# Attention's convolution as products of fp32r high and low parts, in a fused MoE, attention, MoE kernel

## The chip, the cores and the metric

The kernel runs on one NeuronCore of a Trainium2 chip. The metric is device time in microseconds (us) of one execution, lower is better. The engines are TensorE (PE in the profile, its weight loads PEld), VectorE (DVE), ScalarE (ACT), GpSimd (POOL) and SyncE (SP); each works through its own instructions in program order and waits on semaphores for the others.

## The reference

Input x has 2 x 2048 tokens of 256 floats. Three layers follow each other, each on a layer norm of x and each added to x:

```python
x = x + 0.5 * _L0_ffn_ref(_layernorm(x), gate_up_proj, down_proj, router_w)
x = x + _L0_attn_ref(_layernorm(x), conv_w, conv_b, wq, bq, wk, bk, wv, bv, wo, bo, proj_w, proj_b)
x = x + 0.5 * _L0_ffn_ref(_layernorm(x), gate_up_proj, down_proj, router_w)
```

The feed-forward layer is a mixture of 8 experts, two for each token. The attention layer starts with the part that is changed here, a causal convolution over three tokens from 256 channels to 3 x 64 (q, k, v):

```python
xp = jnp.pad(x, ((0, 0), (2, 0), (0, 0)))
qkv = lax.conv_general_dilated(xp, conv_w, window_strides=(1,), padding='VALID',
                               dimension_numbers=('NWC', 'WIO', 'NWC')) + conv_b
q, k, v = jnp.split(qkv, 3, axis=-1)
```

Then come 8 heads of 64 over blocks of 128 tokens with a causal mask, a softmax, an output product and a projection back to 256. All is float32.

## The kernel before

The tokens are 32 tiles of 128, and x stays in SBUF in `x_sb` throughout.

**Expert stages.** Tokens are routed to 71 slots of 128 rows. For each slot a row tile comes in by DMA, PE turns it, ACT copies the turned tile to `rowsT_hi` in the float format fp32r, DVE subtracts that from the exact value into `rowsT_lo`, and PE makes three products: high x high, high x low, low x high. The down product is made in the same way.

**Attention.** `turns(turn)` runs a software pipeline of turns i = -8 to 36, written out by hand for each engine, and every engine goes through its part of turn i in the order of the code. In turn i tile i gets its scores and exponentials, tile i-1 its turned probabilities and context product, tile i-2 its projection, tile i+3 is turned for the convolution, tile i+5 gets the last layer's expert sums (`add_experts`), and tiles from i-5 on are routed for the next expert stage. The convolution works on pairs of tiles. In an odd turn PE makes the q and k channels of the next pair (`qk_pair`, 6 products of 128 x 128 weights with 256 columns, the two channel halves times three taps), and in an even turn the v channels (`v_pair`, 64 weight columns each, the two halves side by side in the array). The moving operand is `xT`, a view into `tile_oh`: 256 columns and 2 further ones ahead of them, the halo, which DVE copies from the pair before. The weights are `conv_sb`, exact float32.

Names that the steps use, in the order in which they come in one turn:

- PE: conv (L1529 q and k, L1538 v), mask and scores into `SS` (L1546, L1551), `prT` = the probabilities turned (L1557), which waits for POOL's `norm`, tile i+3 turned into `A` (L1565), projection `G` (L1594), context `F` (L1605), q and k heads (L1615), v products (L1625), ranks (L1637).
- DVE: `qk` or `vst_lo` (L1236, L1240), four small steps of the rstd, `nmax` (L1259), the routing of `PICKS` turns, residual `x_sb` (L1268), `mhaT` (L1281), halo (L1287), `add_experts` (L934), `qkh` (L1295), `rec` (L1300), statistics (L1309, L1312), `compare` (L1172 to L1178).
- ACT: the rstd seed (L746), `vo`, `hT_sb`, `vst_hi` (L762), `prT` copies (L768), `xT` copy (L777), 8 exponentials (L783).
- POOL: `norm` (L658), which waits for `rec`; gathers of expert results (L666); sends of routed rows (L675).

`PICKS` = {9, 13, 17, 21, 25, ...} are the turns in which four tiles at once get their experts picked on DVE; `compare` comes at the end of the turn before. Ahead of the first turn PE runs `keep_clock(F, 44)`, 44 products that serve nothing but activity. `wprep` counts prepared weights, `first["tokens"]` says that the token table of the first expert stage is done.

## Time and profile before

| | |
|---|---|
| time, median of 3 runs | 769.83 us (769.14 to 770.52) |
| the profiled execution's own time | 768.44 us |
| its span, first to last instruction | 766.7 us |
| mean granted clock of TensorE | 0.959 of full speed |
| PE busy | 684.0 us (89%) |
| DVE busy | 519.3 us (68%) |
| ACT busy | 488.2 us (64%) |
| POOL busy | 336.3 us (44%) |

Starts are in us from the first instruction. The first layer's routing ends at about 80 us, its experts at 230, attention runs from 230 to about 550, then come the last routing and experts. A row of the timeline merges neighbouring instructions of one line ("x12"), and its length is then from the first start to the last end. Matmuls overlap in the pipeline, so a single one's length is longer than the step from one start to the next.

### The profile page before, as it was taken

How to read it: one execution, taken by the hardware profiler on the slowest of the kernel's cores; microseconds unless marked ns; L12 is line 12 of the kernel's file. 1: busy time of each engine (PE TensorE's matmuls, PEld its weight loads, DVE VectorE, ACT ScalarE, POOL GpSimd, SP SyncE). 2: the span in 40 equal slices, each digit the busy share in tenths (PEclk: the TensorE clock that was granted, in tenths of full speed). 3: DMA queues.
4: the chain of work that ended last, by engine and by line, in shares of the span. 5: the costliest groups of instructions: out<-in, count | busy, mean ns of one | idle time of the engine just before them, and what ended most of it. 6: DMA issues, size and time to landing. Idle time of an engine off the chain costs nothing.

```text
span 766.7 us, 19140 instructions
## 1 busy us (share of the span) xinstructions
PE 684.0 (89%) x5321; PEld 587.7 (77%) x5354; DVE 519.3 (68%) x1747; ACT 488.2 (64%) x1735; POOL 336.3 (44%) x361
## 2 busy tenths in 40 slices
PE   4999899999997899999999999999418999999854
PEld 3986799999993677777777777777317999999843
DVE  6578666666664666687878787777654777777653
ACT  4767566666663577777777777767514666666533
POOL 5200544444415544446566665444641445444500
PEclk9999999999998999999999999999757999999968
DMA  9940354544432201112121111100243444444289
GB/s 308 316 136 1 95 150 144 144 132 128 125 100 82 71 28 30 32 32 64 57 66 54 64 57 43 41 32 22 90 112 98 122 133 125 131 124 124 84 302 355
DMA packets 57862, 83.39 MB, mean 109 GB/s; under 512 B 9520, under 2 KB 43827, under 8 KB 57780
## 3 DMA queue, kind: packets, MB, share of 16 engines
q1 hardware_dynamic: 44772, 47.63, 19.9%
q0 software_dynamic: 13008, 34.69, 14.6%
q8 instruction: 48, 0.79, 0.4%
q14 instruction: 34, 0.28, 0.1%
HBM read 45.77 MB, written 37.44 MB: 109 GB/s over the span
## 4 chain that ended last, share of the span: by engine, by line
PE 66%; issue 10%; DVE 8%; POOL 7%; DMA 4%; ACT 3%; SPq 1%; DVEq 0%; POOLq 0%; ACTq 0%
PE CC L1474 18%; PE B L1529 3%; PE CC L1557 3%; POOL yg L666 3%; PE A L1461 3%; PE CC L1615 3%; PE SS L1551 3%; PE F L1605 2%; PE SS L1491 2%; POOL pr L658 2%; PE SS L1492 2%; PE SS L1493 2%; PE F L1625 2%; PE SS L1494 2%; PE SS L1495 2%
## 5 line engine op out<-in xcount | busy, mean ns | idle before, releaser
L630 POOL DMA_INDIRECT shared<-h_rows,tok_i x71 | 66.9, 942 | 116.7 <-DVE tok_i L1071 45.1
L642 POOL DMA_INDIRECT y_rows<-shared,y_dest x71 | 69.8, 984 | 89.1 <-DVE y_dest L1139 75.4
L1474 PE MATMUL CC<-w_hi,rowsT_hi 128*128 x284 | 104.6, 368 | 0.3 <-DVE rowsT_lo L1127 0.2
L658 POOL TENSOR_TENSOR pr<-pr,prec 128x1024 f32<-128x1024 f32 x31 | 58.7, 1893 | 94.9 <-DVE prec L1300 94.9
L1474 PE MATMUL CC<-w_hi,rowsT_lo 128*128 x284 | 92.1, 324 | 0.0
L704 ACT ACTIVATE shared<-CC 128x176 f32<-128x176 f32 x142 | 45.1, 317 | 73.9 <-PE CC L1474 73.9
L1474 PE MATMUL CC<-w_lo,rowsT_hi 128*128 x284 | 92.0, 324 | 0.0
L783 ACT ACTIVATE pr<-SS,nmax 128x128 f32<-128x128 f32 x256 | 90.1, 393 | 1.6 <-DVE nmax L1259 1.6
L1122 DVE TENSOR_TENSOR shared<-shared,CC 128x176 f32<-128x176 f32 x142 | 48.0, 338 | 49.9 <-ACT shared L704 47.6
L675 POOL DMA_INDIRECT h_regions<-h_store,dest x64 | 64.0, 1000 | 38.8 <-DVE dest L1224 21.7
L666 POOL DMA_INDIRECT yg<-y_rows,slot_i x64 | 62.3, 973 | 34.4 <-DMA y_rows<-shared 15.5
L720 ACT ACTIVATE shared<-SS 128x256 f32<-128x256 f32 x142 | 54.5, 384 | 26.0 <-PE SS L1495 24.6
L768 ACT ACTIVATE shared<-CC 128x512 f32<-128x512 f32 x64 | 34.7, 595 | 53.2 <-PE CC L1557 53.2
L783 ACT ACTIVATION_READ_ACCUMULATOR pr<-SS,nmax 128x1 f32 x256 | 59.9, 234 | 0.0
L1474 PEld LDWEIGHTS CC<-w_hi,rowsT_hi 128*128 128x128 f32 x284 | 54.0, 190 | 1.0 <-issue 1.0
L1474 PEld LDWEIGHTS CC<-w_lo,rowsT_hi 128*128 128x128 f32 x284 | 54.5, 192 | 0.0
L1474 PEld LDWEIGHTS CC<-w_hi,rowsT_lo 128*128 128x128 f32 x284 | 54.2, 191 | 0.0
L1491 PE MATMUL SS<-w_hi,hidA_hi 128*128 x142 | 51.8, 365 | 1.0 <-DVE hidB L1133 0.7
L1127 DVE TENSOR_TENSOR rowsT_lo<-A,rowsT_hi 128x256 fp32r<-128x256 f32 x72 | 30.5, 424 | 29.7 <-ACT rowsT_hi L709 29.7
L1529 PE MATMUL B<-tile_oh,conv_sb 128*128 128x256 f32 x192 | 46.0, 390 | 1.4 <-ACT tile_oh L777 1.4
L1127 DVE TENSOR_TENSOR rowsT_lo<-B,rowsT_hi 128x256 fp32r<-128x256 f32 x70 | 29.7, 424 | 20.9 <-ACT rowsT_hi L709 20.8
L1529 PEld LDWEIGHTS B<-tile_oh,conv_sb 128*128 128x128 f32 x192 | 37.6, 196 | 7.9 <-issue 1.8
(312 smaller groups left out, 2003.2 us busy)
## 6 DMA issues: line engine op xcount, KB each, us to landing
shared<-h_regions SPq DMA_DIRECT2D x71, 129.0 KB
y_rows<-shared SPq DMA_DIRECT2D x71, 128.0 KB, 1.7
w_lo<-y_rows SPq DMA_DIRECT2D x9, 512.0 KB, 8.0
x_sb<-in_x_dram SPq DMA_DIRECT2D x8, 512.0 KB, 7.7
out_dram<-x_sb SPq DMA_DIRECT2D x16, 256.0 KB, 6.3
w_hi<-y_rows SPq DMA_DIRECT2D x7, 512.0 KB, 11.7
w_lo<-in_gupT_dram SPq DMA_DIRECT2D x2, 1408.0 KB, 12.9
h_regions<-pad_rows SPq DMA_DIRECT2D x15, 129.0 KB, 2.8
```

Of the source, the lines that this page charges most:

```text
L630: pool.indirect_dma_start(out=rows[:, s % RING, 0:D], out_offset=None, in_=h_dram[:, :], in_offset=bass.IndirectOffsetOnAxis(ap=tok_i[:, s ...
L642: pool.indirect_dma_start(out=y_dram[0:TOPK * TOKENS, :], out_offset=bass.IndirectOffsetOnAxis(ap=y_dest[:, s:s + 1], axis=0), in_=y_sb[:, ...
L658: pool.tensor_tensor(pr[:, q, :, :], pr[:, q, :, :], prec[:, q, :].unsqueeze(2).to_broadcast([P, NH, P]), ALU.mult).then_inc(t["norm"], 1)
L666: pool.indirect_dma_start(out=yg[:, q, k, :], out_offset=None, in_=y_dram[:, :], in_offset=bass.IndirectOffsetOnAxis(ap=slot_i[:, b, k:k + ...
L675: pool.indirect_dma_start(out=h_regions[:, :], out_offset=bass.IndirectOffsetOnAxis(ap=dest[:, q, k:k + 1], axis=0), in_=hr[:, q, :], in_o ...
L720: a.activation(y_sb[:, u % RING, :], SS[:, 512 * (u % 2):512 * (u % 2) + D], ACT.Copy).then_inc(r["y_sb"], 1)
L783: e = a.activation(pr[:, u % 2, h, :], SS[:, h * P:(h + 1) * P], ACT.Exp, bias=nmax[:, u % 2, h:h + 1], accum_out=psums[:, u % 2, h:h + 1])
L1122: v.tensor_tensor(hid[:, p, 0:H], gate[:, p, :], CC[:, 512 * p + H:512 * p + GU], ALU.mult).then_inc(r["hid"], 1)
L1127: v.tensor_tensor(rowsT_lo[:, p, :], (A, B)[p][:, 0:D], rowsT_hi[:, p, :].bitcast(F32), ALU.subtract).then_inc(r["rowsT_lo"], 1)
L1474: i = pe.matmul(CC[:, 512 * (u % 2):512 * (u % 2) + GU], rows_part[:, u % 2, c * P:(c + 1) * P], weights, start=(n == 1), stop=(n == 3 * DC))
L1491: pe.matmul(acc, hidA_hi[:, u % 2, :], w_hi[:, at_a], start=True, stop=False)
L1529: x = pe.matmul(B[:, 0:2 * P], conv_sb[:, c, k * P:(k + 1) * P], xT[:, p % 2, c, k:k + 2 * P], start=(c == 0 and k == 0), stop=(c == DC - ...
```

## The change

The convolution's exact float32 products become sums of fp32r products, as in the expert stages.

- **Weights.** `conv_w` is no longer among the early `loads`. SP loads it once the token table is done, into a free part of `tile_oh`. When the first expert stage has ended, ACT makes `conv_qk_hi` (128 x 768) and the high halves of `conv_v` (2 x 128 x 192), and DVE then the low parts. PE waits for all of them (`wprep` 13) ahead of its filler products.
- **Inputs.** ACT writes `xT_hi` (fp32r) where it wrote `xT`. DVE makes `xT_lo` = `A` - `xT_hi` for each tile, right behind `mhaT`, and in even turns (odd tiles) two halo copies in place of one. Both live in `turned_parts`, memory shared with the expert stages.
- **Products.** q and k: 18 fp32r products of 256 columns in place of 6 float32 ones (each of which is two instructions in the trace, 12 in all). v: 12 fp32r products with 128 weight columns, high and low parts side by side, in place of 6 float32 ones with 64.
- **Waits.** PE waits for `xT_lo` where it waited for `xT_sb` and `halo`. ACT's `hT` copy waits for the `xT_lo` of the turn before.
- **Constants.** `mask_bf` is 128 x 128 and read four times over, where it was 128 x 512.

```diff
-        loads = [(conv_sb[:, :, :], conv_w), (convb_sb[:, 0:1], conv_b[0:2 * W, :]),
+        loads = [(convb_sb[:, 0:1], conv_b[0:2 * W, :]),
...
+            sp.wait_ge(loaded, 16 * len(loads))
+            sp.wait_ge(first["tokens"], 1)
+            sp.dma_start(conv_sb, conv_w).then_inc(loaded, 16)
             store_y(0)
...
-                mask_rows = mask_bf[:, :].rearrange("p (h s) -> p h s", s=P)
-                const_step(pool.affine_select(out=mask_rows, in_=mask_rows, compare_op=ALU.is_ge, fill=MASKED,
-                                              base=0, pattern=[[0, 4], [-1, P]], channel_multiplier=1))
+                const_step(pool.affine_select(out=mask_bf[:, :], in_=mask_bf[:, :], compare_op=ALU.is_ge, fill=MASKED,
+                                              base=0, pattern=[[-1, P]], channel_multiplier=1))
...
                 a.preload_act_table_set("natural_log_exp_and_others")
+                a.wait_ge(loaded, 16 * (len(loads) + 1))
+                a.activation(conv_qk[0][:, :, :], conv_sb_qk, ACT.Copy).then_inc(wprep, 1)
+                for c in range(DC):
+                    a.activation(conv_v_parts[0][:, c, :, :], conv_sb_v[:, c, :, :], ACT.Copy).then_inc(wprep, 1)
...
-                    if there(i + 3) and (i + 3) % 2:
+                    if there(i + 3):
                         b, p = i + 3, (i + 3) // 2
-                        v.wait_ge(t["xT_sb"], b + 1)
-                        after(v, t["conv"], 2 * p)
-                        v.tensor_tensor(xT[:, (p + 1) % 2, :, 0:TAPS - 1], xT[:, p % 2, :, 2 * P:2 * P + TAPS - 1],
-                                        keep[:, b:b + 1].unsqueeze(1).to_broadcast([P, DC, TAPS - 1]), ALU.mult
-                                        ).then_inc(t["halo"], 1)
+                        at_b = TAPS - 1 + b % 2 * P
+                        v.wait_ge(t["xT_hi"], b + 1)
+                        ins = v.tensor_tensor(xT_lo[:, p % 2, :, at_b:at_b + P],
+                                              A[:, 0:D].rearrange("p (c n) -> p c n", c=DC),
+                                              xT_hi[:, p % 2, :, at_b:at_b + P].bitcast(F32), ALU.subtract)
+                        if b % 2:
+                            step(ins)
+                            after(v, t["conv"], 2 * p)
+                            for part in (xT_hi, xT_lo):
+                                ins = v.tensor_tensor(part[:, (p + 1) % 2, :, 0:TAPS - 1],
+                                                      part[:, p % 2, :, 2 * P:XT].bitcast(F32),
+                                                      keep[:, b:b + 1].unsqueeze(1).to_broadcast([P, DC, TAPS - 1]),
+                                                      ALU.mult)
+                        ins.then_inc(t["xT_lo"], 1)
...
+                v.wait_ge(wprep, 7 + 1 + DC)
+                v.tensor_tensor(conv_qk[1][:, :, :], conv_sb_qk, conv_qk[0][:, :, :].bitcast(F32), ALU.subtract
+                                ).then_inc(wprep, 1)
+                for c in range(DC):
+                    v.tensor_tensor(conv_v_parts[1][:, c, :, :], conv_sb_v[:, c, :, :],
+                                    conv_v_parts[0][:, c, :, :].bitcast(F32), ALU.subtract).then_inc(wprep, 1)
                 turns(turn)
...
+                CONV_PARTS = (conv_qk[0], xT_hi), (conv_qk[1], xT_hi), (conv_qk[0], xT_lo)
...
+                        pe.wait_ge(t["xT_lo"], 2 * p + 2)
                         after(pe, t["qkv"], p)
                         pe.sem_inc(passed_pe, 1)
...
+                        for c, k in taps:
+                            for n, (weights, part) in enumerate(CONV_PARTS):
+                                x = pe.matmul(B[:, 0:2 * P], weights[:, c, k * P:(k + 1) * P],
+                                              part[:, p % 2, c, k:k + 2 * P], start=((c, k) == taps[0] and n == 0),
+                                              stop=((c, k) == taps[-1] and n == 2), skip_group_check=True)
...
             pe.wait_ge(const, 5)
+            pe.wait_ge(wprep, 7 + 2 * (1 + DC))
             pe.matmul(G[:, 0:D], ones_r[:, :], projb_parts[:, :], start=True, stop=True).then_inc(projb, 1)
             keep_clock(F[:, :], 44)
             attention()
```

DVE in even turn 12, before, from the residual on (`tile_oh` in the L1287 row is `xT`, `shared` is `qkh`, `prec` is what `rec` makes):

```order
L1268 TENSOR_TENSOR x_sb<-x_sb,G 128x256
L1271 BN_STATS astats<-x_sb 128x6
L1274 BN_AGGR moments<-astats 128x2
L1229 TENSOR_TENSOR lg<-G,zeros 128x8
L1281 TENSOR_TENSOR mhaT<-F,mha_bias 128x128
L1287 TENSOR_TENSOR tile_oh<-tile_oh,keep 128x2x2
L934 SCALAR_TENSOR_TENSOR x_sb<-yg,wts,x_sb 128x256 x2
L1295 TENSOR_TENSOR shared<-CC,bqk_sb 128x1024
L1300 RECIPROCAL prec<-psums 128x8
```

The same place of the changed kernel (`turned_parts` is `xT_lo` and `xT_hi`, and `tile_oh` is now `mhaT`):

```order
L1283 TENSOR_TENSOR x_sb<-x_sb,G 128x256
L1286 BN_STATS astats<-x_sb 128x6
L1289 BN_AGGR moments<-astats 128x2
L1244 TENSOR_TENSOR lg<-G,zeros 128x8
L1296 TENSOR_TENSOR tile_oh<-F,mha_bias 128x128
L1302 TENSOR_TENSOR turned_parts<-A,turned_parts 128x2x128
L1309 TENSOR_TENSOR turned_parts<-turned_parts,keep 128x2x2 x2
L949 SCALAR_TENSOR_TENSOR x_sb<-yg,wts,x_sb 128x256 x2
L1319 TENSOR_TENSOR shared<-CC,bqk_sb 128x1024
L1324 RECIPROCAL prec<-psums 128x8
```

One instruction of 128 x 256 has come in ahead of `add_experts`, `qkh` and `rec`; it stands there in every turn up to tile 31. The second halo copy is there in even turns only.

DVE at the start of attention, changed kernel (L949 is the first `add_experts`, in turn -5):

```order
L1355 MEMSET moments 128x8
L1358 CAST turned_parts<-zeros 128x2x2 x2
L1362 TENSOR_TENSOR conv_qk_lo<-tile_oh,conv_qk_hi 128x768
L1365 TENSOR_TENSOR conv_v<-tile_oh,conv_v 128x3x64 x2
L949 SCALAR_TENSOR_TENSOR x_sb<-yg,wts,x_sb 128x256 x2
L1333 BN_STATS astats<-x_sb 128x6
```

Before, one memset of the halo stood between `moments` and the first `add_experts`. The first `xT_lo` comes in turn -3, right ahead of that turn's (the third) `add_experts`.

ACT at the same place, changed kernel (`tile_oh` as input is the exact `conv_w`, as output the projection bias):

```order
L816 ACT_TABLE_LOAD
L818 ACTIVATE conv_qk_hi<-tile_oh 128x768
L820 ACTIVATE conv_v<-tile_oh 128x3x64 x2
L821 ACTIVATE tile_oh<-zeros 128x40
L823 ACTIVATE tile_oh<-G 128x256
L757 ACTIVATE lnvar<-moments,eps 128x2
```

The three copies of L818 and L820 are new; they stand ahead of the projection bias and of the first seed.

## Rows read from the trace of the kernel before

**Rows 1.** PE's waits from 262 to 540 us, all of attention's full turns

```profile
PE CC L1557 <- POOL pr L658: 3.1, 5, 1.2
```

**Rows 2.** Busy time of the engines by window, with the granted clock behind POOL's

```profile
340.00:400.00 60.00, 58.83 (x554) 46.18 (x559) 44.90 (x142) 44.90 (x171) 39.74 (x34) 1.00 0.18 57
...
244.00:248.00 4.00, 2.51 (x6) 1.80 (x7) 2.82 (x11) 1.39 (x5) 1.89 (x2) 0.50 0.12 33
```

**Rows 3.** PE's timeline in turns 13 and 14: start, length, line

```profile
365.57 2.75 PE L1529 MATMUL B<-tile_oh,conv_sb 128*128 128x256 f32 x12
368.37 0.38 PE L1546 MATMUL SS<-mask_bf,ident_bf 128*128 128x512 bf16 x1
...
369.77 1.09 PE L1557 MATMUL CC<-ident,pr 128*128 128x128 f32 x8
...
375.83 1.51 PE L1538 MATMUL B<-tile_oh,conv_sb 128*64 128x256 f32 x12
...
378.91 0.33 PE L1557 MATMUL CC<-ident,pr 128*128 128x128 f32 x1
```

**Rows 4.** POOL's timeline: the two `norm` that these `prT` wait for

```profile
366.87 1.89 POOL L658 TENSOR_TENSOR pr<-pr,prec 128x1024 f32<-128x1024 f32 x1 [1.59 <-DVE prec L1300]
...
376.96 1.89 POOL L658 TENSOR_TENSOR pr<-pr,prec 128x1024 f32<-128x1024 f32 x1 [3.17 <-DVE prec L1300]
```

**Rows 5.** DVE's timeline in turns 12 and 13

```profile
360.52 0.42 DVE L1240 TENSOR_TENSOR vst_lo<-B,vst_hi 128x256 fp32r<-128x256 f32 x1 [1.63 <-ACT vst_hi L762]
360.86 0.15 DVE L1246 SCALAR_TENSOR_TENSOR at<-arstd 128x2 f32<-128x2 f32 x1
...
362.75 0.42 DVE L1268 TENSOR_TENSOR x_sb<-x_sb,G 128x256 f32<-128x256 f32 x1
363.32 0.43 DVE L1271 BATCH_NORM_STATS2 astats<-x_sb 128x6 f32<-128x256 f32 x1
...
364.24 0.15 DVE L1287 TENSOR_TENSOR tile_oh<-tile_oh,keep 128x4 f32<-128x4 f32 x1
...
372.93 0.41 DVE L1268 TENSOR_TENSOR x_sb<-x_sb,G 128x256 f32<-128x256 f32 x1
```

**Rows 6.** DVE's residual (L1268) in turns 10 to 14: first and last start

```profile
L1268 DVE TENSOR_TENSOR x_sb<-x_sb,G x5: 406/415/423, 345.2 to 381.8; 128x256 f32<-128x256 f32 x5
```

**Rows 7.** DVE's waits from 333 to 488 us, turns 9 to 25: total, times, longest

```profile
DVE vst_lo L1240 <- ACT vst_hi L762: 12.5, 8, 1.6
DVE x_sb L1268 <- PE G L1594: 4.4, 4, 1.1
```

**Rows 8.** PE's timeline in the first expert stage: fp32r products of 256 columns

```profile
200.43 0.28 PE L1492 MATMUL SS<-w_lo,hidA_hi 128*128 x1
200.55 0.28 PE L1493 MATMUL SS<-w_hi,hidA_lo 128*128 x1
```

**Rows 9.** PE's timeline at the start of attention

```profile
231.00 9.44 PE L1514 MATMUL F<-mask_bf,ident_bf 128*128 128x512 bf16 x43
240.91 0.44 PE L1565 MATMUL A<-ident,shared 128*128 128x128 f32 x2 [0.46 <-ACT shared L796]
...
246.18 4.70 PE L1529 MATMUL B<-tile_oh,conv_sb 128*128 128x256 f32 x12 [1.42 <-ACT tile_oh L777]
```

**Rows 10.** ACT's timeline at the start of attention

```profile
230.28 1.28 ACT L805 ACT_TABLE_LOAD   x1
```

**Rows 11.** Splitting copies and subtractions of the expert weights: count, busy us, mean ns

```profile
L838 ACT ACTIVATE w_hi<-w_lo 128x960 fp32r<-128x960 f32 x8 | 8.0, 994 | 0.0
...
L1034 DVE TENSOR_TENSOR w_lo<-w_lo,w_hi 128x960 fp32r<-128x960 f32 x1 | 1.1, 1145 | 0.0
```

**Rows 12.** POOL's timeline in the first layer: the mask's memset

```profile
14.37 0.52 POOL L574 MEMSET mask_bf<- 128x512 bf16 x1
```

**Rows 13.** The chain that ended last, in the first layer

```profile
15.04 0.65 POOL mask_bf L576
```

**Rows 14.** PE's timeline at the first rows of the first expert stage

```profile
81.75 0.44 PE L1461 MATMUL A<-ident,shared 128*128 128x128 f32 x2 [1.15 <-DMA shared<-h_rows,tok_i]
```

More of the change, by code:

```diff
@@ L123, in macaron_kernel @@
         rw_sb = sb("rw_sb", [P, DC * E])
-        conv_sb = sb("conv_sb", [P, DC, TAPS * 3 * W])
+        conv_qk = [sb(f"conv_qk_{part}", [P, DC, TAPS * P], F32R) for part in ("hi", "lo")]
+        conv_v = sb("conv_v", [P, DC, TAPS, 2 * W], F32R)
+        conv_v_parts = conv_v[:, :, :, 0:W], conv_v[:, :, :, W:2 * W]
         convb_sb = sb("convb_sb", [P, 1])
@@ L260, in macaron_kernel @@
         prec = sb("prec", [P, 2, NH])
[L261 removed]
+        mhaT = tile_oh[:, :, :].rearrange("p j n -> p (j n)").bitcast(F32)[:, 2 * P:3 * P]
         eps = sb("eps", [P, 1])
@@ L305, in macaron_kernel @@
             "g0", "g1", "g2", "g3", "combined", "before", "after", "seed", "rstd", "normed", "xT",
-            "xT_sb", "halo", "conv", "qk", "vhi", "qkv", "qkh", "qkh_sb", "vo", "vo_sb", "scores", "max", "exp", "rec",
+            "xT_hi", "xT_lo", "conv", "qk", "vhi", "qkv", "qkh", "qkh_sb", "vo", "vo_sb", "scores", "max", "exp", "rec",
             "norm", "prT", "prT_low", "prT_high", "mha", "mhaT", "out", "res", "routed", "hrT", "hT", "logits", "lg",
@@ L1331, in attention @@
                 st.did(v.memset(moments[:, :, :, :], 1.0))
-                v.memset(xT[:, 0, :, 0:TAPS - 1], 0.0).then_inc(const, 1)
+                v.wait_ge(R[0]["y"], SLOT_TILES + 2)
+                for part in (xT_hi, xT_lo):
+                    ins = v.tensor_copy(part[:, 0, :, 0:TAPS - 1],
+                                        zeros[:, 0:DC * (TAPS - 1)].rearrange("p (c n) -> p c n", c=DC))
+                ins.then_inc(const, 1)
+                v.wait_ge(wprep, 7 + 1 + DC)
[4 more added lines that the diff above has]
+                                    conv_v_parts[0][:, c, :, :].bitcast(F32), ALU.subtract).then_inc(wprep, 1)
                 turns(turn)
@@ L1513, in keep_clock @@
                 for _ in range(n):
-                    pe.matmul(bank, ident_bf[:, :], mask_bf[:, :], start=True, stop=True, skip_group_check=True)
+                    pe.matmul(bank, ident_bf[:, :], mask_4, start=True, stop=True, skip_group_check=True)
             def attention():
                 t = T
+                CONV_PARTS = (conv_qk[0], xT_hi), (conv_qk[1], xT_hi), (conv_qk[0], xT_lo)
+                taps = [(c, k) for c in range(DC) for k in range(TAPS)]
                 def turn(i):
@@ L1535, in turn @@
                         pe.wait_ge(t["qk"], p + 1)
-                        for k in range(TAPS):
-                            for c in range(DC):
-                                x = pe.matmul(B[W * c:W * (c + 1), 2 * P:4 * P],
-                                              conv_sb[:, c, V_AT + k * W:V_AT + (k + 1) * W],
-                                              xT[:, p % 2, c, k:k + 2 * P], start=(k == 0), stop=(k == TAPS - 1),
-                                              skip_group_check=True)
+                        for c, k in taps:
+                            for n, part in enumerate((xT_hi, xT_lo)):
+                                x = pe.matmul(B[:, 2 * P:4 * P], conv_v[:, c, k, :], part[:, p % 2, c, k:k + 2 * P],
+                                              start=((c, k) == taps[0] and n == 0),
+                                              stop=((c, k) == taps[-1] and n == 1), skip_group_check=True)
                         x.then_inc(t["conv"], 1)
@@ L1561, in turn @@
                         pe.wait_ge(t["normed"], b + 1)
-                        after(pe, t["xT_sb"], b)
+                        after(pe, t["xT_lo"], b)
                         after(pe, t["hT"], i - POST + 1)
```

46 lines of the change are left out of this document (22 added, 24 removed).

## The prediction

> **What bounds the kernel now.** I read the windows first: from 340 to 400 us, the middle of attention, PE is busy 58.8 of 60 us and DVE 44.9 [rows 2]. That looks like a stage bound by PE, in which cheaper products pay in full. The waits say less: PE waits little for POOL (3.1 us in 278 us [rows 1]), but a wait that is short can still be one that is just met. So I went through the timelines of two turns and asked at each wait of PE how early the other side was.
>
> The one that matters is `prT`, which waits for POOL's `norm`. In turn 13 the norm ends at 366.87 + 1.89 = 368.76 and `prT` starts at 369.77: 1.0 us to spare. In turn 14 it ends at 378.85 and `prT` starts at 378.91 [rows 3, 4]: nothing to spare, although no wait is booked. The norm waits for DVE's `rec`, and DVE gets to `rec` after `x_sb`, the statistics, `mhaT`, `add_experts` and `qkh`, all in one queue. So half of the turns are bound by DVE and POOL just as much as by PE.
>
> DVE's own waits confirm it. In 155 us, 16 turns, it waits 4.4 us for the projection, in four of the turns, and 12.5 us for `vst_hi` in the eight even turns [rows 7]. The latter is no slack either: ACT makes `vst_hi` behind a seed that waits for DVE's last statistics of the turn before, so it moves with DVE's queue. From `x_sb` of turn 12 to `x_sb` of turn 13 (362.75 to 372.93 [rows 5]) DVE is occupied without a wait for anybody: turn 12 ends with `compare`, turn 13 has the picking. Routing comes back every four turns; such a cycle lasts 381.8 - 345.2 = 36.6 us [rows 6].
>
> **The change, part by part.** The sum is made against the profiled execution's 768.44 us, which is 1.4 us below the median of 769.83; I add the same difference to both.
>
> *Products.* q and k take 2.80 us from conv to mask (365.57 to 368.37), and v's twelve instructions last 1.51 us [rows 3]. An fp32r product of 256 columns with 128 weight columns steps by 0.12 us [rows 8]. So q and k take 18 x 0.12 = 2.16, with the last one's pipeline about 2.25: 0.55 us less. v takes 12 x 0.12 = 1.44: no difference worth counting. That is 0.55 us once in two turns, in the odd ones, where `prT` has its spare time; the even ones gain nothing.
> The Trainium skill (TensorE: Matmul & The Clock Gate, sections "LDWEIGHTS (loading the stationary operand)" and "The mechanism") speaks against this: a load of 128 columns takes about 107 ns, and loads overlap running products only where the row groups differ. By it each product would cost 107 + 107 ns, and q and k 3.8 us instead of 2.25. The rows of 0.12 us, same row groups, contradict it.
>
> *DVE, per tile.* `xT_lo` has the shape and formats of `vst_lo`, behind which the next instruction starts 0.34 us later (360.52 to 360.86 [rows 5]). In odd turns (even tiles) that is all: +0.34. In even turns the halo waits for its completion: `x_sb`, with such a wait behind it, steps 0.57 (362.75 to 363.32), and the second halo copy adds between 0 and its length of 0.15 [rows 5]; I take 0.07, since such small ones overlap. +0.64. The bounds of the two together are 0.68 and 1.14 per pair; I take 0.98.
>
> *What of it is on the path.* One cycle of four turns, from `x_sb` to `x_sb`:
> - Turn 12 to 13, DVE without a wait: +0.64. PE's 0.55 goes into waiting.
> - Turn 13 to 14, `rec` and norm just in time: +0.34.
> - Turn 14 to 15, an odd turn without picking: the norm has 0.6 to 1.0 us to spare, which 0.64 eats up and no more; the product's gain cannot come through either. About +0.05.
> - Turn 15 to 16, like 13 to 14: +0.34.
>
> Together 1.37 us in a cycle. From turn 8, ahead of the first pick turn, to turn 26 there are 4.5 of them: **+6.2**. In turns 1 to 8 there is no picking: an odd turn gives back 1.0 - 0.64, about 0.3, an even one costs 0.34: **0**. After turn 26 `add_experts` has ended and DVE has about 1 us more (its two instructions of 128 x 256); there the products' gain counts in the last of the two convs left, turn 29's: **-0.6**. In turn 27 PE waits for POOL anyway; that is the longest of its waits, 1.2 us [rows 1].
>
> *Start of attention.* Before, PE goes into its fillers at 231.00, they last 9.44, and the first turned tile follows at 240.91 after 0.46 us of waiting [rows 9]: the fillers are just long enough. Now they wait for all weight parts. ACT's table load ends at 231.56 [rows 10]. Then come 1152 elements in three copies and as many in three subtractions; 960 take 0.99 on ACT and 1.15 on DVE [rows 11], so about 1.3 and 1.6 us, one after the other with hand-overs of 0.1: fillers from about 234.9 instead of 231.0 with their bias product ahead, first tile at about 244.4, +3.5. DVE cannot run ahead of it, since the first `xT_lo` (which waits for that tile) stands ahead of the third `add_experts`, and from there statistics, seed, second tile and second `xT_lo` follow each other up to the first conv. That conv runs at a granted clock of 0.50, 1.2 GHz [rows 2], and takes 4.70 us [rows 9]. It will again, since the idle time behind the fillers is about as long as before: 18 x 0.24 = 4.3, 0.4 less. Then one more `xT_lo` up to the first scores, +0.3. Together **+3.4**. Bounds: 0.5, if the fillers' delay were covered, and 4.5.
>
> *Start of the first expert stage.* `conv_w` (590 kB) now comes while PE waits 1.15 us for the first gathered rows [rows 14]. Before it was among the early loads and cost PE nothing visible. Bounds 0 and 2 us (more than the wait itself); the gather's own issue comes later than the load's. **+0.3**.
>
> *Mask.* The memset of 0.52 us and the select of 0.65 us are on the chain that ended last [rows 12, 13], and are a quarter as wide now. Between 0 and 1.17 us of gain, with a fixed part as small instructions have: **-0.6**.
>
> Sum: 6.2 + 0 - 0.6 + 3.4 + 0.3 - 0.6 = +8.7. 768.4 + 8.7 = 777.1 for a profiled execution, 778.5 for the median.
>
> **The rivals.**
> 1. *PE's time is what counts; faster.* For: 98% busy [rows 2]. Against: the norm's end just ahead of `prT` in even turns [rows 4]. If DVE's additions fitted into waits, 15 convs would give 0.55 each: -8.3 + 3.4 + 0.3 - 0.6 = -5.2, 764.6. It decides below about 0.5 us of DVE time on the path per pair of turns. Chance 0.06.
> 2. *The start is covered.* If the weight parts are ready sooner or the chain of the first tiles has slack behind the fillers, the 3.4 falls to about 0.5: 775.6. For: DVE's first `add_experts` waits for its gathers anyway. Against: only 0.46 us between fillers and tile [rows 9]. Chance 0.12.
> 3. *The weight loads show.* An fp32r product with a load of its own at each step could cost what the float32 instructions do, 2.80 / 12 = 0.23 us [rows 3]: q and k 4.2, v 2.8, +2.7 per pair of turns on PE, which then bounds all turns: about 16 x 2.4 + 3 = +41, 811. Taps at odd offsets, which the expert stages don't have, would be a reason. Chance 0.04. By the figures of the Trainium skill above (TensorE: Matmul & The Clock Gate) it would come to nearly the same.
> 4. *DVE's additions cost more than their steps*, since `xT_lo` reads the same PSUM bank that PE and ACT use, or ACT's new wait bites: 0.3 us more per turn, +8, 787. Chance 0.06.
> 5. *The path is bound by DVE in fewer turns*: with 0.7 in place of 1.37 per cycle, 775.3. Chance 0.12.
>
> The forecast itself has 0.60, with 776.5 to 781 as its own range. From 773 to 784 it takes in rivals 2 and 5 as well, and leaves out 0.06 + 0.04 + 0.06 and some tails. 0.2% of the time, 1.5 us, is about what a measurement of this kernel tells from no change. Faster by more: rival 1 and a tail of 2 and 5, 0.07. Within: 0.03. Slower: 0.90.
>
> **What the changed profile would show.** q and k at 2.2 us, v at 1.45. PE busy falling by 0.5 us a pair, and its waits for POOL at `prT` rising from 3 us to some 15. DVE's cycle of four turns at 38.0 us where it was 36.6, `add_experts` 0.34 and 0.64 later behind `mhaT`. Fillers starting near 235, the first conv near 249.7 and still at half clock. The first expert rows about as before. Wrong would be: `prT` of even turns waiting no longer than now, or a conv above 2.8 us.

## The result, and the profile after

The changed kernel takes 780.4 us (median of 4 runs, 779.38 to 782.8) against 770.0 for the kernel before, run beside it: a ratio of 1.0144 with a 95% interval of 1.0123 to 1.0164. The forecast was 778.5 and slower. The profiled execution took 779.67 us, its span is 777.9, and the mean granted clock is 0.958.

In the changed kernel the lines of turns are: PE conv L1564 and L1573, mask L1580, `prT` L1591, xT transposes L1599, v products L1659; DVE `vst_lo` L1255, `x_sb` L1283, `mhaT` L1296, `xT_lo` L1302, halo L1309; POOL `norm` L669. The page, with what answers to the busy table and the chain (before, PE had 66% of the chain and DVE 8%):

```profile
PE 681.9 (88%) x5450; PEld 598.6 (77%) x5450; DVE 536.0 (69%) x1799; ACT 491.4 (63%) x1738; POOL 336.8 (43%) x361
...
PE 52%; DVE 20%; issue 9%; POOL 7%; ACT 5%; DMA 4%; SPq 2%; DVEq 0%; POOLq 0%; ACTq 0%
```

The same 60 us of attention as in [rows 2]; PE's waits in the turns, as in [rows 1], here from 265 to 550 us; and DVE's `x_sb` over the same four turns, as in [rows 6]:

```profile
340.00:400.00 60.00, 55.49 (x554) 46.11 (x554) 47.91 (x156) 43.81 (x167) 35.30 (x31) 1.00 0.17 52
```

```profile
PE CC L1591 <- POOL pr L669: 10.0, 19, 1.7
```

```profile
L1283 DVE TENSOR_TENSOR x_sb<-x_sb,G x5: 406/415/423, 352.6 to 390.3; 128x256 f32<-128x256 f32 x5
```

PE is busy 3.3 us less in the window and DVE 3.0 more, PE waits for `norm` 19 times where it waited 5 times, and four turns take 37.7 us where they took 36.6. So one engine was made cheaper and now waits for another that was made dearer.

PE's timeline in turn 13 of the changed kernel, from the first product of q and k to `prT` (the pairs between repeat the pattern), and then v in turn 14:

```profile
373.20 0.28 PE L1564 MATMUL B<-turned_parts,conv_qk_hi 128*128 128x256 f32 x1
373.32 0.28 PE L1564 MATMUL B<-turned_parts,conv_qk_lo 128*128 128x256 f32 x1
...
375.35 0.60 PE L1580 MATMUL SS<-mask_bf,ident_bf 128*128 128x512 bf16 x2
...
377.00 1.09 PE L1591 MATMUL CC<-ident,pr 128*128 128x128 f32 x8
...
383.68 1.68 PE L1573 MATMUL B<-turned_parts,conv_v 128*128 128x256 f32 x12
385.20 0.60 PE L1580 MATMUL SS<-mask_bf,ident_bf 128*128 128x512 bf16 x2
```

q and k take 373.20 to 375.35 = 2.15 us (2.80 in [rows 3]), v 1.52 (1.51). POOL's `norm` for this `prT` starts at 375.05, lasts 1.89 and so ends at 376.94, 0.06 ahead of 377.00: the 1.0 us that turn 13 had to spare is gone. In every turn from 1 to 27 of the changed kernel `prT` starts 0.05 to 0.06 us behind the end of its norm.

```profile
375.05 1.89 POOL L669 TENSOR_TENSOR pr<-pr,prec 128x1024 f32<-128x1024 f32 x1 [2.12 <-DVE prec L1324]
```

DVE's timeline in turns 12 and 13, where the additions are, as in [rows 5]:

```profile
371.69 0.28 DVE L1296 TENSOR_TENSOR tile_oh<-F,mha_bias 128x128 f32<-128x128 f32 x1
371.88 0.41 DVE L1302 TENSOR_TENSOR turned_parts<-A,turned_parts 128x256 fp32r<-128x256 f32 x1
372.33 0.24 DVE L1309 TENSOR_TENSOR turned_parts<-turned_parts,keep 128x4 fp32r<-128x4 f32 x2
372.49 1.00 DVE L949 SCALAR_TENSOR_TENSOR x_sb<-yg,wts,x_sb 128x256 f32<-128x256 f32 x2
...
382.39 0.28 DVE L1296 TENSOR_TENSOR tile_oh<-F,mha_bias 128x128 f32<-128x128 f32 x1
382.58 0.41 DVE L1302 TENSOR_TENSOR turned_parts<-A,turned_parts 128x256 fp32r<-128x256 f32 x1
382.92 1.00 DVE L949 SCALAR_TENSOR_TENSOR x_sb<-yg,wts,x_sb 128x256 f32<-128x256 f32 x2
```

In the odd turn the new instruction costs 382.92 - 382.58 = 0.34 us. In the even turn subtraction and halos together take 372.49 - 371.88 = 0.61. Before, the one halo copy began at 364.24 [rows 5] and the step behind it at 364.31, 0.07 later, so 0.54 us were added there:

```profile
364.31 1.00 DVE L934 SCALAR_TENSOR_TENSOR x_sb<-yg,wts,x_sb 128x256 f32<-128x256 f32 x2
```

The start of attention, PE's timeline as in [rows 9], and the granted clock there (it stands behind POOL's busy time):

```profile
235.83 0.55 PE L1714 MATMUL G<-projb_parts,ones_r 128*128 128x256 f32 x1 [4.76 <-DVE conv_v L1365]
236.18 12.13 PE L1548 MATMUL F<-mask_bf,ident_bf 128*128 128x512 bf16 x44
248.15 0.38 PE L1599 MATMUL A<-ident,shared 128*128 128x128 f32 x2
...
253.38 0.55 PE L1564 MATMUL B<-turned_parts,conv_qk_hi 128*128 128x256 f32 x1 [3.42 <-DVE turned_parts L1309]
```

```profile
236.00:240.00 4.00, 4.00 (x10) 1.44 (x11) 1.40 (x3) 0.38 (x1) 3.09 (x4) 0.50 0.34 99
240.00:244.00 4.00, 4.00 (x17) 1.71 (x16) 2.32 (x9) 1.51 (x5) 3.09 (x4) 0.86 0.35 101
```

The fillers start 5.2 us later and take 12.13 us instead of 9.44 (for the 43 of the 44 that the trace before shows; all 44 take 9.67 in a run below): after a wait of 4.76 us their first 4 us run at a granted clock of 0.50, which is 1.2 GHz, and only 10 of them fit in.

The start of the first expert stage, PE's timeline as in [rows 14], and the window behind it, changed and then before:

```profile
81.78 0.44 PE L1495 MATMUL A<-ident,shared 128*128 128x128 f32 x2 [1.90 <-DMA shared<-h_rows,tok_i]
```

```profile
84.00:90.00 6.00, 6.00 (x34) 5.79 (x33) 3.21 (x10) 2.81 (x11) 3.08 (x4) 0.72 0.28 79
```

```profile
84.00:90.00 6.00, 6.00 (x44) 5.73 (x43) 3.78 (x12) 3.29 (x14) 4.43 (x5) 1.00 0.38 108
```

PE waits 1.90 us for the first gathered rows where it waited 1.15, and then runs at a granted clock of 0.72 over the six microseconds from 84, with 34 instructions in it. Before there were 44 and the clock was 1.00. POOL's gather of these rows shows where the longer wait comes from, before and changed:

```profile
78.95 0.97 POOL L630 DMA_INDIRECT shared<-h_rows,tok_i  x1 [45.09 <-DVE tok_i L1071]
```

```profile
78.25 0.97 POOL L641 DMA_INDIRECT shared<-h_rows,tok_i  x1 [44.55 <-DVE tok_i L1086]
```

From the gather to the first rows on PE it is 3.53 us (78.25 to 81.78) where it was 2.80 (78.95 to 81.75): the rows take 0.7 us longer. The gather itself starts 0.7 us earlier, and this hides the loss at the first product of slot 0.

How far the changed kernel is behind at each place (starts of the same instruction in the two traces):

| place | behind by, us | step, us | forecast |
|---|---|---|---|
| first product of slot 0 | -0.2 | -0.2 | -0.6 (mask) |
| slots 3 to 69 of the first expert stage | 1.25 | +1.4 | +0.3 (load) |
| `prT` of turn 1 (263.23 and 270.44) | 7.2 | +6.0 | +3.4 |
| `x_sb` of turn 8 | 6.5 | -0.7 | 0 |
| `x_sb` of turn 26 | 12.3 | +5.8 | +6.2 |
| `x_sb` of turn 31 | 11.8 | -0.5 | -0.6 |
| end of the span (766.7 and 777.9) | 11.1 | -0.6 | 0 |

### The profile page after: what moved, and what is told of

Same layout as the page of the kernel before. It is cut to its first block, busy times and chain, and to the rows that moved or that the text cites. A ratio compares the mean times of both kernels' runs of the same rounds, so it can differ in the third digit from the quotient of the medians.

```text
span 777.9 us, 19405 instructions
## 1 busy us (share of the span) xinstructions
PE 681.9 (88%) x5450; PEld 598.6 (77%) x5450; DVE 536.0 (69%) x1799; ACT 491.4 (63%) x1738; POOL 336.8 (43%) x361
## 4 chain that ended last, share of the span: by engine, by line
PE 52%; DVE 20%; issue 9%; POOL 7%; ACT 5%; DMA 4%; SPq 2%; DVEq 0%; POOLq 0%; ACTq 0%
PE CC L1508 18%; POOL pr L669 3%; PE A L1495 3%; DVE shared L1319 2%; DVE nmax L1274 2%; PE SS L1525 2%; PE SS L1526 2%; PE SS L1527 2%; PE SS L1528 2%; PE SS L1529 2%; POOL h_regions L686 2%; PE B L1495 2%; DVE x_sb L949 2%; POOL yg L677 2%; PE CC L1591 2%
## 5 line engine op out<-in xcount | busy, mean ns | idle before, releaser
L1508 PE MATMUL CC<-w_hi,turned_parts 128*128 x568 | 173.3, 346 | 0.2 <-DVE turned_parts L1142 0.2
L1508 PEld LDWEIGHTS CC<-w_hi,turned_parts 128*128 128x128 f32 x568 | 104.3, 190 | 1.1 <-issue 0.8
L669 POOL TENSOR_TENSOR pr<-pr,prec 128x1024 f32<-128x1024 f32 x31 | 58.7, 1895 | 99.4 <-DVE prec L1324 99.3
L1508 PE MATMUL CC<-w_lo,turned_parts 128*128 x284 | 92.1, 324 | 0.0
L1508 PEld LDWEIGHTS CC<-w_lo,turned_parts 128*128 128x128 f32 x284 | 54.3, 191 | 0.0
L1525 PE MATMUL SS<-w_hi,turned_parts 128*128 x142 | 51.7, 364 | 1.0 <-DVE turned_parts L1148 0.7
L1142 DVE TENSOR_TENSOR turned_parts<-A,turned_parts 128x256 fp32r<-128x256 f32 x72 | 30.6, 424 | 29.5 <-ACT turned_parts L720 29.5
L1591 PE MATMUL CC<-ident,pr 128*128 128x128 f32 x256 | 35.8, 284 | 10.3 <-POOL pr L669 10.0
L1142 DVE TENSOR_TENSOR turned_parts<-B,turned_parts 128x256 fp32r<-128x256 f32 x70 | 29.7, 425 | 21.0 <-ACT turned_parts L720 21.0
L1319 DVE TENSOR_TENSOR shared<-CC,bqk_sb 128x1024 f32<-128x1024 f32 x32 | 39.2, 1224 | 5.3 <-PE CC L1649 0.8
L1564 PE MATMUL B<-turned_parts,conv_qk_hi 128*128 128x256 f32 x192 | 38.7, 290 | 4.3 <-DVE turned_parts L1309 4.3
## 6 DMA issues: line engine op xcount, KB each, us to landing
w_hi<-y_rows SPq DMA_DIRECT2D x7, 512.0 KB, 11.7
```

Source lines behind the costliest of these rows:

```text
L669: pool.tensor_tensor(pr[:, q, :, :], pr[:, q, :, :], prec[:, q, :].unsqueeze(2).to_broadcast([P, NH, P]), ALU.mult).then_inc(t["norm"], 1)
L1142: v.tensor_tensor(rowsT_lo[:, p, :], (A, B)[p][:, 0:D], rowsT_hi[:, p, :].bitcast(F32), ALU.subtract).then_inc(r["rowsT_lo"], 1)
L1319: v.tensor_tensor(qkh[:, :, :], CC[:, :].rearrange("p (m n) -> p m n", n=P), bqk_sb[:, :, :].rearrange("p a m -> p (a m)").unsqueeze(2) .t ...
L1508: i = pe.matmul(CC[:, 512 * (u % 2):512 * (u % 2) + GU], rows_part[:, u % 2, c * P:(c + 1) * P], weights, start=(n == 1), stop=(n == 3 * DC))
L1525: pe.matmul(acc, hidA_hi[:, u % 2, :], w_hi[:, at_a], start=True, stop=False)
```

## The experiments

They are to tell apart who sets the turns (DVE's additions, or PE's products), why the start costs 6 us, and why PE is slow at 84 us. Four of them were run first on a chip on which the kernel before takes 810 us, then again on a quick one.

### Four kernels on a chip on which each takes over 800 us

The edits are shown with the second run of each, below. What was expected of the first runs:

**Fillers ahead of the wait.**

> Only the wait for the eight weight-part instructions moves: behind the 44 filler products instead of ahead of them, the first convolution waits for them. Theory (the late fillers are the whole of the start term: 4.8 us of waiting and 2.7 us of fillers at half clock): the fillers start as soon as the first expert stage has ended, take 9.4 us again, hide the making of the parts, and the first tile's transposes come 6.0 us earlier: 774.4 us, 1.0057 of the kernel before. Rival A (the wait alone is won, the fillers still run slow): 775.6 us at best. Rival B (the turns after it wait for something else that the late start had hidden, such as DVE at the end of the weight parts): under 3 us won, 777.5 us or more.

**The load later.**

> Only the load of the convolution's weights moves: behind the first loop of stores of the first expert stage instead of beside its first gather. Theory (the load delays the first gathered rows by 0.75 us, TensorE waits 1.9 us instead of 1.15 and is granted half clock for the products of the next slot or two): the granted clock in 84 to 100 us is 1.00 again instead of 0.89, the gate-and-up products of slot 3 stand at before's time, and 779.1 us is measured (1.3 less than the changed kernel's 780.4). Rival (the clock falls for another reason, say the end of the low parts, which now runs at another time): slot 3 stays 1.2 us late, 780.4 us.

**The kernel before with one subtraction more per tile.**

> The kernel before with one more VectorE instruction per tile, the subtraction of a 128 x 256 tile at the place where the changed kernel has it, into an unused target; ScalarE and TensorE wait for it as in the changed kernel. Everything else is before's. Theory (VectorE sets the turns, TensorE's convolution does not): 32 subtractions of which some 19 to 27 lie on the path at 0.34 to 0.39 us, less the small halo waits: plus 6 us, 776 us, and a cycle of four turns of 37.7 to 38.0 us instead of 36.6. Rival (TensorE sets the turns, and the growth in the changed kernel comes from its products and their waits): plus 1 us or less, 771 us, cycle 36.6 us.

**No low part of the turned tiles.**

> The changed kernel without the low part of the turned tiles: VectorE neither subtracts it nor copies its halo, and the products that read it read the high part in its place (so this part of the sum is left out of the result), in the same number and shape. Weight parts, fillers and load stay. Theory (VectorE's additions are the growth in the turns, the shorter convolution gives 0.55 us twice a cycle only where VectorE waits for it): the turns give back their 5.8 us and 0.5 to 1.1 us per cycle more, the start and the first stage stay late by 7.2 us: 772 to 775 us, cycle 35.5 to 36.6 us. Rival (TensorE's products are the growth, since 18 and 12 products cost more in place than 6 of four passes): the cycle stays at 37.7 us and the time at 779 to 780 us.

Measured against 810.1 for the kernel before: 0.9991 (0.9967 to 1.0014), 1.0038 (1.0014 to 1.0062), 1.0016 (0.9985 to 1.0046) and 0.9931 (0.9905 to 0.9957). Single runs of one kernel spread by 5 to 9 us, and one more lay 4 us above these. All four ratios lie below what the theory gave, by more than their intervals, the third stands where its rival had it, and the fourth kernel is faster than the kernel before, clear of noise; so nothing is built on these sums. The waits of PE show what differs, here for the fourth kernel, first on this chip and then on the quick one:

```profile
PE F L1657 <- issue: 24.8, 16, 6.0
PE CC L1589 <- POOL pr L669: 5.1, 8, 1.5
```

```profile
PE F L1657 <- issue: 6.0, 7, 2.2
PE CC L1589 <- POOL pr L669: 4.1, 8, 1.6
```

`issue` is a wait for which the profile names nothing; the expectations call it a wait for instructions, which no run here shows. At the v products it is 24.8 us in 16 waits instead of 6.0 in 7. Waits of that size can cover what DVE does; that they did was not tested. Only what lies ahead of turn 8 was read: in the first of the four the fillers took 9.67 us at a granted clock of 1.00, as in its second run below.

### The changed kernel again

> The changed kernel again, unedited, since the first four experiments ran on a chip on which the kernel before takes 810 us and every kernel has long waits for instructions in the attention turns. If the chip of this call is a quick one (kernel before at 770 us), the ratio should be 1.014 again, as first measured. If it is the slow one, theory: the growth in the turns is hidden in part by the waits for instructions that TensorE has there in either kernel, and the ratio is 1.004 to 1.010; rival: the additions and those waits do not overlap, and the difference stays 10 to 11 us, 1.013.

A quick chip: 780.7 us (780.56 to 781.2) against 769.6, ratio 1.0133 (1.0102 to 1.0164). Its trace repeats the table above to 0.2 us up to turn 31 (7.1 at turn 1, 6.4, 12.2, 11.7). Only the last stage differs, and the span ends 12.8 us late instead of 11.1; so the last line of the table is no property of the change.

### DVE's time alone: the kernel before plus one subtraction

```diff
+                    if there(i + 3):
...
+                        v.wait_ge(t["xT_sb"], b + 1)
+                        v.tensor_tensor(spare_lo, A[:, 0:D].rearrange("p (c n) -> p c n", c=DC),
+                                        xT[:, p % 2, :, at_b:at_b + P], ALU.subtract).then_inc(halo, 1)
                     if there(i + 3) and (i + 3) % 2:
```

PE (before it overwrites the turned tile) and ACT wait for this count as they do in the changed kernel. Convolution, weights and load are those of before.

> The same kernel as the one of before with one subtraction more per tile, hoped for on a chip on which the kernel before takes 770 us. On the slow chip its first seven turns grew by 1.0 us against its own first turn (tile transposes at plus 6.2 in the first, plus 7.2 in the seventh), then waits for instructions took over. Theory: plus 5 to 7 us, ratio 1.007 to 1.009, cycle of four turns 37.6 to 38.0 us. Rival (TensorE sets the turns): plus 1 us or less, ratio under 1.002.

775.8 us against 768.9, ratio 1.0078 (1.0059 to 1.0098), and over four turns:

```profile
L1272 DVE TENSOR_TENSOR x_sb<-x_sb,G x5: 408/414/422, 347.6 to 385.1; 128x256 f32<-128x256 f32 x5
```

37.57 us a cycle, 1.0 more than before, which is three times 0.34: the odd turn without picking absorbs the fourth. From turn 8 to turn 26 this kernel falls behind by 4.8 us. The theory holds; PE has the same products as before and waits for `norm` 13 times instead of 5. This kernel also has the new waits of PE and ACT; that the time and not these waits is what counts, the subtraction made twice shows below.

### PE's time alone: no low part of the turned tiles

```diff
-                        ins = v.tensor_tensor(xT_lo[:, p % 2, :, at_b:at_b + P],
-                                              A[:, 0:D].rearrange("p (c n) -> p c n", c=DC),
-                                              xT_hi[:, p % 2, :, at_b:at_b + P].bitcast(F32), ALU.subtract)
...
-                            for part in (xT_hi, xT_lo):
+                            for part in (xT_hi,):
...
-                CONV_PARTS = (conv_qk[0], xT_hi), (conv_qk[1], xT_hi), (conv_qk[0], xT_lo)
+                CONV_PARTS = (conv_qk[0], xT_hi), (conv_qk[1], xT_hi), (conv_qk[0], xT_hi)
```

All 30 products of a pair stay, but those with the low part read the high part, so the result leaves the low part out.

> The same kernel as the one without the low part of the turned tiles (the products read the high part in its place), hoped for on a quick chip. Theory: the start and the first stage stay late by 7.1 us against before, the turns give back their 5 us and 0.5 to 1.1 us per cycle of four more: 1 to 5 us over the kernel before (771 to 775 us), ratio 1.001 to 1.006, where the changed kernel has 1.013 to 1.014. Rival: 1.012 or more.

769.6 us, ratio 1.0000 (0.9988 to 1.0013): a little better than the 771 to 775 us that the theory gave, and 11 us under the changed kernel's. The profiled execution took 772.3, the longest of ten.

```profile
L1283 DVE TENSOR_TENSOR x_sb<-x_sb,G x5: 406/416/423, 350.4 to 386.6; 128x256 f32<-128x256 f32 x5
```

36.15 us a cycle: 0.4 under before, 1.6 under the changed kernel. So the shorter convolution is worth 0.4 us in four turns, once, in the odd turn without picking (turns 11, 15, 19, 23), and DVE's additions are worth 1.6. From turn 8 to 26 it gains 2.0 us on the kernel before, and in turns 1 to 8 another 1.9. The rival, PE's products as the growth, is out.

### Dose: the subtraction twice

```diff
                         v.wait_ge(t["xT_hi"], b + 1)
+                        v.tensor_tensor(spare_lo, A[:, 0:D].rearrange("p (c n) -> p c n", c=DC),
+                                        xT_hi[:, p % 2, :, at_b:at_b + P].bitcast(F32), ALU.subtract)
```

> The changed kernel with the low part of each turned tile subtracted twice, the first time into an unused target, 32 more VectorE instructions of 128 x 256. Theory (in the changed kernel VectorE sets nearly every turn from the eighth to the twenty-sixth): 0.29 to 0.34 us for each of 19 to 27 tiles on the path, 5.5 to 9 us more than the changed kernel in the same call, cycle of four turns 38.9 us or more instead of 37.7. Rival (GpSimd's scaling of the scores is what TensorE waits for, and VectorE has slack again behind it): under 2 us more.

788.7 us where the changed kernel, run beside it, has 780.7: 8.0 more, a ratio of 1.0239 (1.0205 to 1.0273) to the kernel before. The cycle goes to 39.15 us, 1.43 more, 0.36 for each instruction, now with no turn that absorbs anything, and with no wait added:

```profile
L1285 DVE TENSOR_TENSOR x_sb<-x_sb,G x5: 407/414/423, 356.3 to 395.4; 128x256 f32<-128x256 f32 x5
```

### The start: fillers ahead of the wait

```diff
             pe.wait_ge(const, 5)
-            pe.wait_ge(wprep, 7 + 2 * (1 + DC))
             pe.matmul(G[:, 0:D], ones_r[:, :], projb_parts[:, :], start=True, stop=True).then_inc(projb, 1)
             keep_clock(F[:, :], 44)
+            pe.wait_ge(wprep, 7 + 2 * (1 + DC))
```

> The same kernel as the one with the fillers ahead of the wait, hoped for on a quick chip. On the slow one its fillers took 9.7 us, at full clock, and its first tile came 5.8 us earlier in relation to the end of the first expert stage than in the changed kernel. Theory: 774 to 775 us, ratio 1.005 to 1.007. Rival: part of it is lost again in the first turns (the shift fell by 0.7 us there in the changed kernel, so slack may exist), 776 us or more, ratio 1.008 or more.

775.2 us, ratio 1.0072 (1.0052 to 1.0091):

```profile
231.66 9.67 PE L1548 MATMUL F<-mask_bf,ident_bf 128*128 128x512 bf16 x44
241.81 0.41 PE L1599 MATMUL A<-ident,shared 128*128 128x128 f32 x2 [0.48 <-ACT shared L807]
...
248.50 0.55 PE L1564 MATMUL B<-turned_parts,conv_qk_hi 128*128 128x256 f32 x1 [3.17 <-DVE turned_parts L1309]
```

The fillers are at full clock and the first tile comes 0.9 us behind before's, of which 0.6 is from the first stage: the 6 us are gone at that place. But the first conv comes 6.7 us after the first tile (before 5.3, [rows 9]), since the low part of the first tiles stands in DVE's queue among `add_experts` and seeds; at turn 1 the kernel is 2.3 us behind before's, 1.7 more than at the end of the first stage, where the changed kernel has 6.0. So of 6.0 us, 4.3 were the late fillers. The 1.7 that stay fall to 0.6 where DVE's additions are moved (below). I had expected all 6.0 from this edit.

### The load later

```diff
-            sp.wait_ge(loaded, 16 * len(loads))
-            sp.wait_ge(first["tokens"], 1)
-            sp.dma_start(conv_sb, conv_w).then_inc(loaded, 16)
             store_y(0)
```

The three lines stand behind the first loop of `store_y(0)` instead.

> The same kernel as the one with the weight load moved behind the first stores, hoped for on a quick chip. In the combined kernel with this edit the granted clock in 84 to 90 us was 1.00 (0.72 in the changed kernel) and slot 3 stood 1.6 us earlier than in the changed kernel. Theory: 1.2 to 1.7 us less than the changed kernel, 778.7 to 779.3 us, ratio 1.011 to 1.012, and the wait for the first gathered rows is 1.1 us instead of 1.9. Rival (another edit of the combined kernel did that): 1.013 to 1.014 and a clock of 0.72 there.

778.2 us, ratio 1.0117 (1.0095 to 1.0139), and PE's first rows and the window:

```profile
80.95 0.44 PE L1495 MATMUL A<-ident,shared 128*128 128x128 f32 x2 [1.16 <-DMA shared<-h_rows,tok_i]
```

```profile
84.00:90.00 6.00, 6.00 (x45) 5.75 (x44) 4.26 (x13) 3.88 (x16) 3.94 (x5) 1.00 0.40 113
```

The wait is back at 1.16, the clock at 1.00, and slots 3 to 69 stand 0.8 us ahead of before and 2.1 ahead of the changed kernel. That the load lengthens the wait is shown: in all seven traces with the load beside the gather, on either chip, 3.5 to 3.8 us pass from the gather to the first rows on PE, and 2.7 to 2.8 in all seven without. The clock is less settled. All five traces of quick chips with the load beside the gather wait 1.9 to 2.0 us and then have the lower clock, four of the five without it don't; but the fifth, the kernel before with a subtraction more, whose first stage is that of before, shows a wait of 1.19 us and the lower clock nevertheless:

```profile
80.82 0.44 PE L1469 MATMUL A<-ident,shared 128*128 128x128 f32 x2 [1.19 <-DMA shared<-h_rows,tok_i]
```

```profile
84.00:90.00 6.00, 6.00 (x36) 5.88 (x34) 3.44 (x10) 3.07 (x12) 3.06 (x4) 0.76 0.30 81
```

On the slower chip the two did not go together: the kernel without a low part waited 2.19 us there and kept 1.00 from 84 to 90 us, the one with the load later waited 1.15 and had 0.83. So the load makes the loss of 1.4 us behind the wait likely and is not its only way in; that the wait brings the lower clock is not shown. The Trainium skill (TensorE: Matmul & The Clock Gate, "What's actually happening") says that one kernel meets the clock gate differently from run to run; these traces, one of each kernel, neither confirm nor exclude that as the reason. The same loss is in the kernel before with a subtraction more. Its profiled execution ends 7.9 us behind before's: 1.0 ahead at slot 0, then 1.5 lost in the first stage, 0.6 up to turn 1, 0.5 in turns 1 to 8, 4.8 in turns 8 to 26, and 1.4 behind them. So 5.9 us lie where the subtraction is, and the 6.9 in the medians are not all its own.

### All together: the low part moved

Fillers first, load later, and on DVE:

```diff
+                    if i % 2 == 0:
+                        low(i + 3)
...
                         v.bn_aggr(moments[:, u % 2, 0, :], astats[:, 0, :]).then_inc(t["before"], 1)
+                    if i % 2:
+                        low(i + 3)
+                    elif there(i + 3):
+                        b, p = i + 3, (i + 3) // 2
+                        v.wait_ge(t["xT_lo"], b + 1)
+                        after(v, t["conv"], 2 * p)
...
+                        ins.then_inc(halo, 1)
```

`low(b)` is the subtraction of tile b with its wait. In odd turns it comes last, where DVE then waits for `vst_hi` ([rows 5] show 1.63 us); the two halo copies come last in even turns, with a count of their own.

> Fillers ahead of the wait for the weight parts, the load of the convolution's weights behind the first stores of the first expert stage, in odd turns the low part made at the end of the turn (where VectorE otherwise waits), and the two halo copies at the end of the even turns, counted apart. Theory (all that was added on VectorE's path but one subtraction in the even turns is gone, and the shorter convolution gives 0.55 us twice a cycle where VectorE waits for it): the start term of 6.0 us and the first-stage term of 1.2 us go, and the turns cost 0 to 3 us over the kernel before: ratio 0.999 to 1.004 where the changed kernel has 1.014. Rival (the low part made late holds the next tile's transposes and so the next convolution, TensorE waits there instead): the turns stay at plus 5 us or more, ratio 1.007 or more.

768.7 us against 769.6, ratio 0.9992 (0.9974 to 1.0010): no difference that can be told from the kernel before, and 12.0 us under the changed one. The cycle is 37.05 us. The start costs 0.6 us at turn 1, turns 8 to 26 cost 2.8. The rival, a late low part that holds PE, did not come.

The last kernel has, beside all this, the halo copies on GpSimd, behind `norm`, and not on DVE:

```diff
+                    if i % 2 and there(i + 2):
+                        b, p = i + 2, (i + 2) // 2
+                        pool.wait_ge(t["xT_lo"], b + 1)
+                        after(pool, t["conv"], 2 * p)
...
+                        for part in (xT_hi, xT_lo):
+                            ins = pool.tensor_tensor(part[:, (p + 1) % 2, :, 0:TAPS - 1],
...
+                        ins.then_inc(halo, 1)
```

> As the kernel with the low part moved, with the two halo copies on GpSimd behind its scaling of the scores in the odd turns instead of on VectorE. Theory (VectorE gets back 0.3 to 0.5 us in half of the turns, and GpSimd, busy 15 of 40 us to 26 of 40 us in the turns, has room): 1 to 3 us less than that kernel, ratio 0.996 to 1.001. Rival (the scaling of the scores is what TensorE waits for, and the copies put off the gathers behind them, which then land late): the same as that kernel or slower by up to 4 us.

766.5 us, ratio 0.9958 (0.9937 to 0.9979): this version beats both kernels, 3.1 us under the kernel before and 14.2 under the changed one.

```profile
365.36 1.89 POOL L670 TENSOR_TENSOR pr<-pr,prec 128x1024 f32<-128x1024 f32 x1 [1.85 <-DVE prec L1331]
367.21 0.35 POOL L679 TENSOR_TENSOR turned_parts<-turned_parts,keep 128x4 fp32r<-128x4 f32 x2
367.71 1.02 POOL L689 DMA_INDIRECT yg<-y_rows,slot_i  x1
```

```profile
L1304 DVE TENSOR_TENSOR x_sb<-x_sb,G x5: 411/414/423, 343.8 to 380.2; 128x256 f32<-128x256 f32 x5
```

On POOL both copies take 0.35 us and put the gather off by as much; from 262 to 540 us no wait of DVE for a gather is in the trace. The cycle is 36.46 us, 0.1 under before: with all the low parts made, only here does the cheaper convolution pay for them in the turns. Turns 1 to 8 gain 1.9 us on the kernel before, as with no low part at all.

The cycles in one view, by what was changed on DVE and on PE (each is the last start less the first of `x_sb` in turns 10 to 14; the changed kernel's next three cycles take 38.0, 38.0 and 37.7 us):

| kernel | cycle, us | ratio to before |
|---|---|---|
| before [rows 6] | 36.6 | 1 |
| shorter conv, no low part | 36.15 | 1.0000 (late start) |
| low part moved, halos on POOL | 36.46 | 0.9958 |
| low part moved | 37.05 | 0.9992 |
| before's conv, one subtraction more | 37.57 | 1.0078 |
| the changed kernel | 37.72 | 1.0133 |
| changed, subtraction twice | 39.15 | 1.0239 |

## Why the prediction was right, and where its sizes were off

- **Who sets the turns.** Right. It took PE's 98% busy as no proof, since `norm` ended just ahead of `prT` in even turns [rows 3, 4]. One DVE instruction of 0.34 us per tile, with PE untouched, costs 4.8 us in turns 8 to 26 and 1.0 us in a cycle; the products with no DVE time give back 0.4 us in a cycle. Rival 1 needed the opposite, rival 3 needed q and k at 4.2 us and got 2.15. There the rows of 0.12 us [rows 8] decided rightly. The Trainium skill (TensorE: Matmul & The Clock Gate, "The mechanism") says that weight loads overlap running products only where the row groups differ. The trace does not agree: 18 products started at 373.20, 373.32 and so on, on the same row groups, also with taps at odd offsets.
- **The size in the turns.** Right by its steps. `x_sb` falls behind by 0.54 us from turn 12 to 13 (forecast 0.64: the subtraction with the wait for its completion took 0.45 us, 371.88 to 372.33, and not 0.57), 0.34 from 13 to 14 (0.34), -0.06 from 14 to 15 (0.05), 0.66 from 15 to 16 (0.34); the last is 0.33 in some other cycles. +5.8 against +6.2. Rivals 4 and 5 are out.
- **Turns 1 to 8.** -0.7 against 0. The experiment without a low part shows 1.9 us of gain from the conv there, 0.4 to 0.6 in each of turns 3, 5, 7 and 8; in the changed kernel the odd turns give back 0.4 to 0.6, more than the 0.3 that I had left after DVE's part.
- **The start.** The mechanism was right, the term was mis-sized: +3.4 against +6.0. Rival 2, a covered start, is out. The fillers' start was forecast at about 234.9; it was 236.18 with 1.25 of that from the first stage, so 234.9. The step that failed was to carry over the fillers' 9.44 us [rows 9] to a PE that had waited 4.76 us: their first 4 us ran at half clock and they took 12.13. I had looked at the clock of the first conv (right, 0.50 again) and not at that of the fillers. With fillers first, 4.3 us of it went, and of the 1.7 that stayed 1.1 went with DVE's additions, where the forecast had +0.3.
- **The first expert stage.** The table gives +1.4 against +0.3, but that is the loss behind the wait alone, at the lower clock, which the forecast did not have. The longer wait itself, 0.75 us, is lost ahead of slot 0, in the row of the mask. So the load's term was about 2.2 us where the forecast had 0.3, with bounds of 0 to 2; the kernel with the load later stands 2.1 us ahead in these slots.
- **The mask.** -0.6 was put in; the first gather started 0.7 us early, and 0.4 to 1.6 early in the other kernels with the new mask. The kernel before with one subtraction more, which has the old mask, started it 0.97 early on one chip and 0.05 late on the other. So the mask's worth stays open.
- **What was to be seen.** PE's waits at `prT` went from 3.1 to 10.0 us, not to 15; the cycle to 37.7, in two of the four to the 38.0 forecast; the first conv came at 253.4, not near 249.7.
- **The sum.** The profiled execution is 11.2 us longer than before's where the forecast had 8.7. Start, load and mask came 4.1 us dearer; the turns came 1.0 us cheaper and the last stage 0.6, and this last is luck, since the same program run again lost 1.1 us there. The median lies inside the range, near its upper end.

## What to carry to other kernels

When an engine is above 95% busy, look at each of its cross-engine waits for how early the other side was before calling it the bound: here most of what was taken from PE went into waiting, and of four instructions added to DVE three or all four counted. An exchange of work from a busy engine to a second one paid here only when the added instructions stood where the second engine waits anyway, or on a third one; the same products went from 1.4% slower to 0.4% faster by where the subtractions, the halo copies, one load and one wait stand. And the wait put ahead of the filler products cost twice, once itself and once in the clock of the fillers: put the fillers ahead of the wait.

## What the runs showed of the hardware that I had not expected

- After 4.76 us without work PE's next products ran at a granted clock of 0.50 for the whole of the next 4 us although it was busy all the time, and 44 products took 12.13 us instead of 9.67. After a wait of 1.00 us the same 44 ran at 1.00.
- The same program on two chips: span 770.6 and 804.3 us for the kernel without a low part, of which PE's `issue` waits between 262 and 580 us are 6.7 and 27.3 us (6.0 and 24.8 at the v products alone), and the kernel before at 768.9 and 810.1. The four kernels keep their order on the slower chip, but against the kernel before each ratio is 0.6 to 0.8% lower there (0.9931 to 1.0038, on the quick chip 1.0000 to 1.0117): a difference of 1% against that kernel did not carry over from one chip to the other. Why it did not stays open.
- Two copies of 128 x 4 on GpSimd took 0.35 us together, and the gathers behind them moved by as much without a loss in the turns.
